# Attention: a unit's sum over keys moved ahead of the unit's turnings of probabilities

## The reference, cut to what matters

```python
q = (xn @ q_w + q_b).reshape(Bx, Tx, H, -1)        # 4 batches, 1024 rows, 16 heads of 32
k = (xn @ k_w + k_b).reshape(Bx, Tx, H, -1)
att = jnp.einsum('bnhl,bmhl->bnmh', q, k)
att = att + (1.0 - mask) * -1000000.0
att = jax.nn.softmax(att, axis=2)
y = jnp.einsum('bnmh,bmhl->bnhl', att, v).reshape(Bx, Tx, Dx)
```

## Time and profile before

| what | us |
|---|---|
| median of 3 runs | 6470.33 (6466.44 to 6471.92) |
| the profiled execution | 6471.62 |
| its span, first to last instruction | 6469.7 |
| attention, first score matmul to the store of the last y | 488.6 to 1551.8 |

### The profile page before, as it was taken

How to read it: one execution, slowest core, us unless ns; L and a number is a source line. 1 busy time by engine, 2 the same in 40 slices (tenths; PEclk the granted TensorE clock), 3 DMA queues, 4 the chain that set the end, 5 groups by cost and what they waited for, 6 DMA issues and landing times. The chain is left out here.

```text
span 6469.7 us, 86028 instructions
## 1 busy us (share of the span) xinstructions
PE 5565.7 (86%) x30592; PEld 3526.7 (55%) x30592; DVE 4686.6 (72%) x5716; ACT 4209.5 (65%) x6218; POOL 2483.9 (38%) x1098
## 2 busy tenths in 40 slices
PE   6999999998899989996688888887999578888884
PEld 2446666665355544443666666653444366666662
DVE  2328999996455445544999999974554699999993
ACT  1217888885222235554989898964555699999992
POOL 0000000000000000001999999970000499999994
PEclk8999999999999989997999999998999799999997
DMA  5335333332411033334556565633433655555654
GB/s 199 138 134 118 79 86 79 86 76 73 169 43 49 27 108 146 146 133 155 152 150 169 150 168 158 164 85 110 148 143 134 182 148 156 158 154 157 160 149 174
DMA packets 566989, 842.79 MB, mean 130 GB/s; under 512 B 102552, under 2 KB 241944, under 8 KB 566564
## 3 DMA queue, kind: packets, MB, share of 16 engines
q1 hardware_dynamic: 555108, 811.99, 42.9%
q0 software_dynamic: 5120, 16.78, 0.8%
q10 hardware_dynamic: 6336, 8.52, 0.4%
HBM read 544.27 MB, written 292.84 MB: 129 GB/s over the span
## 5 line engine op out<-in xcount | busy, mean ns | idle before, releaser
L1844 POOL TENSOR_TENSOR scan_hC<-scan_h,scan_Crep 128x1024 f32<-128x1024 f32 x1024 | 2395.6, 2367 | 2448.5 <-DVE scan_h L2077 2422.7
L2008 ACT ACTIVATE scan_a<-scan_dt,scan_A 128x512 f32<-128x512 f32 x2048 | 1367.9, 697 | 90.8 <-DVE scan_h L2077 73.3
L1878 PE MATMUL scan_y<-ident,scan_hC 128*128 128x128 f32 x8192 | 1111.6, 279 | 301.0 <-POOL scan_hC L1844 295.4
L1878 PEld LDWEIGHTS scan_y<-ident,scan_hC 128*128 128x128 f32 x8192 | 901.4, 141 | 691.0 <-POOL scan_hC L1844 643.1
L2077 DVE TENSOR_TENSOR_SCAN scan_h<-scan_a,scan_carry,scan_h 128x512 f32<-128x512 f32 x1024 | 1216.9, 1261 | 16.3 <-ACT scan_a L2008 13.1
L2077 DVE TENSOR_TENSOR_SCAN scan_h<-scan_a,scan_h 128x512 f32<-128x512 f32 x1024 | 1155.7, 1200 | 58.8 <-ACT scan_a L2008 58.4
L1984 ACT COPY scan_h<-scan_drive 128x1024 f32<-128x1024 f32 x1024 | 1042.0, 1018 | 166.1 <-PE scan_drive L1866 151.8
L1866 PE MATMUL scan_drive<-scan_Bd,scan_dT 128*128 128x256 f32 x4096 | 749.0, 305 | 126.5 <-ACT scan_h L1984 75.1
L1866 PEld LDWEIGHTS scan_drive<-scan_Bd,scan_dT 128*128 128x128 f32 x4096 | 557.4, 192 | 178.6 <-issue 94.6
L795 DVE CUSTOM_DVE_ANT_0 att_sm<-att_S,att_mneg 128x1024 f32<-128x1024 f32 x512 | 621.9, 1215 | 16.4 <-POOL att_mneg L721 16.1
L853 ACT ACTIVATE att_pr<-att_sm,att_nmax 128x1024 f32<-128x1024 f32 x512 | 590.7, 1154 | 57.8 <-DVE att_nmax L795 45.4
(11 more groups left out here) (189 smaller groups left out, 6256.2 us busy)
## 6 DMA issues: line engine op xcount, KB each, us to landing
scan_dT<-scratch_dtuT SPq DMA_DIRECT2D x512, 256.0 KB, 5.5
scratch_dtuT<-ssmin_dT SPq DMA_DIRECT2D x128, 512.0 KB, 3.5
scan_Crep<-scratch_bc SPq DMA_DIRECT2D x64, 1024.0 KB, 9.3
att_q<-scratch_q_split SPq DMA_DIRECT2D x256, 128.0 KB, 4.3
att_k<-scratch_k_split SPq DMA_DIRECT2D x256, 128.0 KB, 4.5
scratch_uD<-ssmin_uD SPq DMA_DIRECT2D x64, 512.0 KB, 3.4
scratch_z<-ssmin_zt SPq DMA_DIRECT2D x128, 256.0 KB, 2.1
scratch_dt<-ssmin_dt SPq DMA_DIRECT2D x64, 512.0 KB, 2.6
```

What stands on the lines that cost most here:

```text
L1844: nc.gpsimd.tensor_tensor(hC[k % 2][:], of, Crep[:, 2 * p:2 * p + 2, :], ALU.mult).then_inc(s["scaled"].handle, 1)
L1878: last = nc.tensor.matmul(y[j][:, t, :], hC[k % 2][:, i, t * P:(t + 1) * P], ident[:], start=(p == 0 and i == 0 and t == 0), stop=False, i ...
L2008: nc.scalar.activation(a[(2 * k + i) % 3][:], dt[j][:], ACT.Exp, scale=A[:, m, 2 * p + i:2 * p + i + 1]).then_inc(s["decayed"].handle, 1)
```

## The change

In TensorE's list, the two `weigh` of an odd unit come between `scores(u + 3)` and `turn(u)`, and no longer behind `turn(u)`. No instruction is added or removed, and no wait is changed. `turn_back` stays where it was, at the end of the step.

```diff
             for u in range(U + PAIRS + 2):
                 if u + 3 < U:
                     scores(u + 3)
-                if u < U:
-                    turn(u)
                 if u >= PAIRS and u // PAIRS <= G and u % 2 == 1:
                     weigh(u // PAIRS - 1, u % PAIRS - 1)
                     weigh(u // PAIRS - 1, u % PAIRS)
+                if u < U:
+                    turn(u)
                 if u >= 2 * PAIRS and u % PAIRS == 1:
                     turn_back(u // PAIRS - 2)
```

## The result

The changed kernel takes 6624.32 us (median of 4 runs, 6615.38 to 6630.74) against 6469.39 us for the kernel before (4 runs). It is slower by 154.9 us, a ratio of 1.0239 with a 95% interval of 1.0221 to 1.0256. The forecast was 6615 with a range of 6562 to 6665.

The account below looks back on a forecast made before the run. TensorE was taken as full but tied in a ring with VectorE and ScalarE; the closed chain makes each pair 4.67 us against 4.09, 250 times, 144.6 us more, so 6615 us, range 6562 to 6665.

Parts of the forecast that it names:

- a ring with little slack: TensorE, VectorE and ScalarE wait for each other; the 2.95 us chain was covered by about 3.4 us on TensorE.
- the chain that would close: From an odd turning through VectorE's right copy and shift to scores, then sum and next odd turning: 4.67 us a pair.
- The terms: Turning to right copy 1.13, copy to shift 0.61, shift to scores 1.27, scores to sum 0.66, sum to turning 1.00 us.
- scores to sum: On TensorE, start to start: 0.66 us, from a 0.73 record less 0.07 at a change of width; lower end 0.57.
- turn(o) to scores(o + 4): TensorE's step from an odd unit's turning to the next scores, taken as 1.04 us within 2.41 to scores(o + 5).
- The first rival: Shift is done in time anyway, TensorE's steps set the pair at 3.98 to 4.07 us: 6454 to 6477 us; chance 0.08.
- the lower end of the range: With 1.07 for turning to copy and 0.57 for scores to sum: pair 4.52 us, time 6577; range from 6562.
- What was said to be hidden: Turning back (0.19 us), VectorE's once-a-group work and ScalarE's YT copy lie beside the chain and add no time.
- The fall of the clock: Second rival: new gaps pull TensorE's clock to 1.2 GHz, 7235 us if it lasts, some 6675 for a tenth; chance 0.04.

Follow-up runs that it names:

- a shorter link: Changed kernel with VectorE and ScalarE exchanging halves of TP, so VectorE's copy can start after four of eight transposes: 6513.97 us.
- the ring opened on VectorE: Changed kernel with shift(u + 2) ahead of take_right(u - 1) in VectorE's list: 6504.37 us, 1.0049 of the kernel before.
- Opened on TensorE: Changed kernel with the scores moved behind the sum, giving sum, scores, turning: 6469.18 us, 0.9996 of the kernel before.

## Why the prediction was right

- The bound. The prediction read a TensorE that was busy 98.8% of the time as one link of a ring with little slack, and named the chain that would close. The rows after show that chain link by link. The edits bear it out: a copy in the chain cost 89 us (88 expected) and the same copy beside it 4 (0 to 20), a shorter link gave back 110 (107), and the ring opened on VectorE took 6504 us (6500). Opened on TensorE, it gave the whole loss back, but not the 20 us expected on top.
- The terms. Forecast 1.13, 0.61, 1.27, 0.66 and 1.00 us, 4.67 in sum; measured 1.13 (1000.74 to 1001.87), 0.61, 1.28, 0.66 and 1.00, 4.68. Four of the five came from places in the old trace where the chain stood bare or the order happened to be the new one, at the start and the end of the stage. The one that no row showed, scores to sum, came out at 0.66, by the argument that a step after a change of width starts 0.07 ahead of the modelled end. The Trainium skill's "TensorEngine Tiling (Array Packing)" (section "Key Properties") says that a change of tiling mode drains TensorE. The trace nearly agrees: the sum starts 0.66 behind scores whose record is 0.74 long. Since ends are modelled, whether TensorE is empty by then stays open.
- What was taken wrongly, without weight for the forecast. For turn(o) to scores(o + 4) the prediction used 1.04, which is turning to sum; it is 0.85. So TensorE's own steps between turn(o) and scores(o + 5) are 0.85 + 0.58 + 0.79 = 2.22 us and not 2.41, and the wait is 0.47 where about 0.4 was said. The first rival's pair would then have been 3.79 to 3.88 in place of 3.98 to 4.07: by TensorE's steps alone this order would have been faster than the one before. And 0.57 for scores to turning, from which the lower end of the range was built, is not the least that can be: behind a turning back the kernel before has 0.55 (1010.18 in the earlier trace rows to the row here).

```profile
1010.73 1.04 PE L745 MATMUL att_TP<-ident,att_pr 128*128 128x128 f32 x8
```

- What the 9 us beyond the forecast are. 250 x (4.67 - 4.09) was 145 us, the period shows 149. Most of the extra is in one pair out of four, where the scores start 0.15 behind the shift's last record (1013.06 to 1013.21) in place of 0.06:

```profile
1012.98 0.08 DVE L795 DVE_READ_ACCUMULATOR2_ANT att_nmax<- 128x1 f32 x1
...
1013.21 0.70 PE L734 MATMUL att_S<-att_k,att_q 128*128 128x512 f32 x2 [0.57 <-DVE att_nmax L795]
```

  Four such pairs follow each other in sixteen, which is how the scores with one more wait ahead of them lie, the one for a new head's q and k. From 520 to 1680 us the trace has it so: 60 such scores start 0.15 behind, all the others that wait 0.05 to 0.06. That this wait is the reason was not tried. The rest up to 154.9 us is within the spread of the runs.
- What was said to be hidden was hidden: the turning back, `take`, and ScalarE's YT copy lie beside the ring, with four pairs and the one late start explaining the whole period (4 x 4.68 + 0.07 = 18.79).
- The rivals. "The shift is done in time anyway" failed: scores wait 251 times. The fall of the clock didn't happen: 1.00 in the middle of attention, with TensorE idle 0.48 us in each pair. The Trainium skill's "TensorE: Matmul & The Clock Gate" (section "A second HAM failure mode: psum-queue depth-cycling") tells of another kernel, in which short idle times between groups of matmuls made the clock swing. That is not borne out here, with 1.00 beside 251 such waits.
- What missed in the time stood in an expectation, not in the forecast: the gain of 20 us from a sum ahead of the scores, which `take` used up until it was moved too.

## What to carry to other kernels

When engines run written lists and wait for each other, ask of a moved step not only what it waits for, but between which two other steps it used to stand: it may have been the work that covered a chain through another engine. Compare each chain's length with the time that the list leaves between its two ends, on odd and even units apart, since an order with a period of two units can cover one and not the other. The first and last few iterations of a pipelined loop can show the new order's distances before it is built, as they did here.

## What the runs showed that I had not expected

The same 0.42 us of VectorE work cost 89 us behind odd units and nothing that can be told from the spread behind even ones (3.8 us), on an engine that was idle for 4 us in every group. And a group's small steps can eat a gain of their own size: `take`, 0.6 us once in a group, kept the sum-scores-turning order from its whole gain (0.9996 of the kernel before, then 0.9974) until it stood one step later.
